# Re-timing the durations from which a two-layer transformer kernel works out each engine's order

## The reference

```python
def layer(x, c, wmod, attn, ffn):                        # twice, with different attn and ffn
    sa, ca, ga, sb, cb, gb = (silu(c) @ wmod).reshape(16, 6, 1, 128)   # per batch; ga, gb kept off 0
    x = x + ga * attn(layernorm(x) * (1 + ca) + sa)
    return x + gb * ffn(layernorm(x) * (1 + cb) + sb)

attn0(h): Q, K, V = h @ Wq + bq, ...                     # 16 heads of 8
          gate = tanh(gelu(gelu(LN(h @ dp_w1)) @ dp_w2 ...) @ g_w2)    # one number a token
          return ((softmax(causal(Q K^T * scale)) * gate) @ V) @ Wo + bo
ffn0(x):  x = x + softmax(q k^T / sqrt(128)) v @ Wo + bo               # over 128 tokens
          gates = softmax(x @ Wg + bg)                                 # 8 experts, all used
          return x + sum_e gates[e] * (relu(x @ W1[e] + b1[e]) @ W2[e] + b2[e])   # 128 -> 512 -> 128
attn1(x): q, k, v = x @ qkv_w.T;  k, v = layernorm per head
          att = q @ (k^T v / 256 * temperature + attn_bias) + x
          return gelu(att @ p1_w.T + b) @ p2_w.T + b + x
ffn1(x):  top 2 of softmax(x @ w_router); the first 1024 tokens of each expert e:
          y = gelu(x @ w1[e]) @ w2[e];  out[token] += weight * y;  return out + bias
```

## Time and profile before

| | |
|---|---|
| median of 3 runs | 1013.37 us (1011.25 to 1015.28) |
| the profiled execution | 1019.3 us, its span 1017.5 us |
| instructions | 17,056 |
| busy TensorE / VectorE / ScalarE / GpSimd | 936.2 / 608.9 / 567.8 / 347.9 us |
| granted TensorE clock, mean | 0.963 of full speed |

### The profile page before, as it was taken

How to read it: one execution, slowest core, us unless ns; L and a number is a source line. 1 busy time by engine, 2 the same in 40 slices (tenths; PEclk the granted TensorE clock), 3 DMA queues, 4 the chain that set the end, 5 groups by cost and what they waited for, 6 DMA issues and landing times.

```text
span 1017.5 us, 17056 instructions
## 1 busy us (share of the span) xinstructions
PE 936.2 (92%) x6324; PEld 628.5 (62%) x6324; DVE 608.9 (60%) x1747; ACT 567.8 (56%) x965; POOL 347.9 (34%) x436
## 2 busy tenths in 40 slices
PE   4599889888988999999999999999999998988997
PEld 3355555545656787656666566666666666877983
DVE  8988778577475675355554535554455764747334
ACT  4477876775774565445465455545555565453430
POOL 4446540330000000233424443243533323457671
PEclk9599999989997999999999999999999998998999
DMA  5865342643593000101101111111101213112316
GB/s 136 205 156 133 101 122 66 157 123 141 123 226 125 23 22 3 43 21 52 53 22 63 42 40 44 47 37 42 62 21 53 73 47 97 44 50 72 107 46 227
DMA packets 86398, 83.10 MB, mean 82 GB/s; under 512 B 9202, under 2 KB 72680, under 8 KB 86316
## 3 DMA queue, kind: packets, MB, share of 16 engines
q1 hardware_dynamic: 81092, 73.32, 26.1%
q0 software_dynamic: 4320, 8.27, 2.5%
q10 hardware_dynamic: 904, 0.42, 0.1%
HBM read 50.53 MB, written 31.72 MB: 81 GB/s over the span
## 4 chain that ended last, share of the span: by engine, by line
PE 56%; DVE 13%; issue 10%; ACT 9%; SPq 5%; POOL 5%; DMA 2%; another core or an unknown queue 0%; POOLq 0%; DVEq 0%; ACTq 0%
PE psum L1454 13%; PE psum L1487 12%; PE psum L1477 4%; PE psum L1309 4%; PE psum L1247 3%; PE psum L1263 2%; PE psum L1290 2%; POOL routed L2691 2%; SPq L1091 2%; ACT ew L2323 1%; PE psum L1217 1%; PE psum L1239 1%; POOL hT L2633 1%; DVE maxes L1844 1%; PE psum L1368 1%
## 5 line engine op out<-in xcount | busy, mean ns | idle before, releaser
L2432 ACT ACTIVATE big<-psum,cols 128x512 f32<-128x512 f32 x256 | 173.8, 689 | 162.7 <-PE psum L1454 152.1
L1454 PE MATMUL psum<-parts,q_stack 128*128 128x512 f32 x640 | 260.2, 488 | 4.2 <-issue 2.3
L1487 PE MATMUL psum<-big,ew 128*128 128x512 f32 x512 | 249.5, 595 | 0.0
L2633 POOL TENSOR_TENSOR hT<-hT,gb_tok 128x512 f32<-128x512 f32 x56 | 73.6, 1315 | 289.5 <-DVE gb_tok L1965 289.1
L1454 PEld LDWEIGHTS psum<-parts,q_stack 128*128 128x128 f32 x640 | 113.4, 194 | 61.7 <-issue 50.1
L1844 DVE TENSOR_REDUCE maxes<-psum 128x4 f32<-128x1024 f32 (+1 forms) x96 | 114.8, 1218 | 27.6 <-PE psum L1263 27.3
L1487 PEld LDWEIGHTS psum<-big,ew 128*128 128x128 f32 x512 | 96.1, 190 | 53.2 <-issue 39.9
L1454 PE MATMUL psum<-parts,k_stack 128*128 128x512 f32 x320 | 127.5, 398 | 0.0
L1965 DVE SCALAR_TENSOR_TENSOR gb_tok<-psum,cols,gb_tok 128x512 f32<-128x512 f32 x64 | 47.9, 749 | 92.4 <-PE psum L1487 84.7
L2714 POOL DMA_INDIRECT answers<-hT,to x64 | 62.5, 976 | 54.7 <-DVE hT L2163 38.0
L2691 POOL DMA_INDIRECT routed<-big,slot_i x64 | 63.2, 988 | 41.8 <-DVE slot_i L2143 22.2
(11 more groups left out here) (401 smaller groups left out, 1656.2 us busy)
## 6 DMA issues: line engine op xcount, KB each, us to landing
gb_tok<-gate_rows SPq DMA_DIRECT2D x32, 512.0 KB
q_stack<-q_pieces SPq DMA_DIRECT2D x32, 192.0 KB, 3.5
k_stack<-k_pieces SPq DMA_DIRECT2D x32, 192.0 KB, 4.5
routed<-empty_row SPq DMA_DIRECT2D x4, 1040.0 KB, 13.4
big<-routed SPq DMA_DIRECT2D x16, 260.0 KB
answers<-gb_tok SPq DMA_DIRECT2D x4, 1024.0 KB, 11.1
q_pieces<-gb_tok SPq DMA_DIRECT2D x16, 192.0 KB, 2.1
k_pieces<-gb_tok SPq DMA_DIRECT2D x15, 192.0 KB, 2.1
```

The source lines that it names most:

```text
L1454: last = eng.matmul(bank(i), w1_part(wp, e)[:, fs], parts[2 * xk + xp][:, :], start=n == 0, stop=n == 2)
L1487: eng.matmul(bank(i), ew2[:, e, f, :], hid[:, r, f, :], start=f == 0, stop=f == FC - 1).then_inc(sem("down", "pe"))
L2432: eng.activation(hid[:, held("hid", "up", n, e, f), f, :], bank(held("bank", "up", n, e, f)), ACT.Relu, bias=col("L0_ffn_b1", e * FC + f)) ...
L2633: eng.tensor_tensor(hT[:, ns], xpT[:, ns] if e == 0 else hT[:, ns], gate_wide[:, e // GHELD % 2, e % GHELD, :], ALU.add).then_inc(sem("acc ...
```

## The change

Only the `work=` durations of `order_steps()` are changed, and with them the order. Instructions, ranks, urgencies, needs and pools stay. Typical lines, and those that matter below (one line of each kind):

```diff
-        p.step("gv_g", n, work="act:2", urgent=4 if n else 8, after=[("gv_a", n)], tmp=tile)
+        p.step("gv_g", n, work="act:3.2", urgent=4 if n else 8, after=[("gv_a", n)], tmp=tile)
...
-        p.step("gv_h", n, work="act:.35", urgent=4 if n else 8, after=[("gv_d", n)], tmp=tile)
+        p.step("gv_h", n, work="act:2.9", urgent=4 if n else 8, after=[("gv_d", n)], tmp=tile)
...
-        p.step("gv_t", n, work="act:1.6", urgent=4 if n else 8, after=[("gv_r", n)])
+        p.step("gv_t", n, work="act:.35", urgent=4 if n else 8, after=[("gv_r", n)])
...
-            p.step("sg_m", l, n, work="pe:.9 act:.5", after=[("sg_r", l, n)], opens=[(0, bank)], rank=MOE - 100,
+            p.step("sg_m", l, n, work="pe:.45 act:.6", after=[("sg_r", l, n)], opens=[(0, bank)], rank=MOE - 100,
...
-                p.step("up", n, e, f, work="pe:.75 act:.6", after=[("sx", n), ("sw", 0, e), last_pv]
+                p.step("up", n, e, f, work="pe:.765 act:.72", after=[("sx", n), ("sw", 0, e), last_pv]
...
-            one("la_1", b, "pe:.43 act:.7", [("la_a", b)], rank + b, chain, kh, [ka], src=ka)
+            one("la_1", b, f"pe:.42 act:{1.75 if b % BPC == 0 else .5}", [("la_a", b)], rank + b, chain, kh, [ka], src=ka)
...
-        p.step("rt_e", g, work="act:.25", after=[("rt_s", g)], rank=rank, chain=chain)
+        p.step("rt_e", g, work="act:1.55", after=[("rt_s", g)], rank=rank, chain=chain)
...
-        p.step("rt_w", g, work="dve:1.3", after=[("rt_c", g)], rank=rank, chain=chain, urgent=1, closes=[(0, slots)], slots=slots)
+        p.step("rt_w", g, work="dve:1.75", after=[("rt_c", g)], rank=rank, chain=chain, urgent=1, closes=[(0, slots)], slots=slots)
...
-        p.step("fetch", u, work="sp:.5 dma:2.5", after=[("rt_d", b) for b in range(here)] + ([("ans", u - RINGS)] if u >= RINGS else []))
+        p.step("fetch", u, work="sp:.5 dma:3.5", after=[("rt_d", b) for b in range(here)] + ([("ans", u - RINGS)] if u >= RINGS else []))
...
-        p.step("ans", u, work="dve:1.3", after=[("down2", u, CT - 1), *[("rt_b", b) for b in range(RINGS * CHUNK // S)]]
+        p.step("ans", u, work="dve:1.75", after=[("down2", u, CT - 1), *[("rt_b", b) for b in range(RINGS * CHUNK // S)]]
```

More of the change, by code:

```diff
@@ L402, in order_steps @@
         bank = p.buffer("bank")
-        p.step("val", b, work="pe:1.2 dve:.55" if b < 4 else "pe:.75 dve:.48", urgent=6 if b < 4 else 0, after=[("ln_t", 0, 0, b), ("center",)] + ([(("proj", 0, 1), "pe")] if b < BPC else []),
+        p.step("val", b, work="pe:1.2 dve:.55" if b < 4 else "pe:.83 dve:.53", urgent=6 if b < 4 else 0, after=[("ln_t", 0, 0, b), ("center",)] + ([(("proj", 0, 1), "pe")] if b < BPC else []),
                rank=60 * (b - 3) + 4,
@@ L582, in order_steps @@
         split = p.buffer("parts")
-        p.step("sx", n, work="act:.53 dve:.62", after=[("mx_a", b) for b in range(BPC * n, BPC * n + BPC)]
+        p.step("sx", n, work="act:.6 dve:.69", after=[("mx_a", b) for b in range(BPC * n, BPC * n + BPC)]
                + ([(("up", n - 1, NE - 3, FC - 1), "pe")] if n else []),
@@ L599, in order_steps @@
                        opens=[(0, bank)] if f == 0 else [], closes=[(0, hid)] if f == FC - 1 else [], bank=bank, hid=hid)
-            p.step("mix", n, e, work="dve:.7", after=[("down", n, e, FC - 1), ("mg_r", n, e // GHELD)],
+            p.step("mix", n, e, work="dve:.78", after=[("down", n, e, FC - 1), ("mg_r", n, e // GHELD)],
                    closes=[(0, bank)], bank=bank)
-            p.step("acc", n, e, work="pool:1.25", after=[("mix", n, e)] + ([("acc", n, e - 1)] if e else []))
+            p.step("acc", n, e, work="pool:1.4", after=[("mix", n, e)] + ([("acc", n, e - 1)] if e else []))
         add_mixed(n, MOE - 300, (20 + n, -1, 0))
@@ L605, in order_steps @@
     for e in range(NE):
-        p.step("sw", 1, e, work="act:.53 dve:.62", after=[("w1",), (("up", NCH - 1, e, FC - 1), "pe")])
+        p.step("sw", 1, e, work="act:.6 dve:.69", after=[("w1",), (("up", NCH - 1, e, FC - 1), "pe")])
     for h in range(4):
@@ L632, in linear_attention @@
             chain, (kq, kk, ks, kb, ka, kh, ko) = (20 + n, b, 2), tiles[b]
-            p.step("la_m", b, work="dve:.65", after=[("la_r", n)], rank=rank + b, chain=chain, closes=[(0, ks)], src=kk)
+            p.step("la_m", b, work="dve:.93", after=[("la_r", n)], rank=rank + b, chain=chain, closes=[(0, ks)], src=kk)
             if b < B - LAST:
@@ L678, in order_steps @@
             bank = p.buffer("bank")
-            p.step("up2", u, f, work="pe:.77 act:.52", after=[("ft", u), ("sw", 1, e)] + ([(("up2", u, f - 1), "pe")] if f else []), rank=at + f,
+            p.step("up2", u, f, work=f"pe:.77 act:{1.9 if u < 2 and f == 0 else .64}", after=[("ft", u), ("sw", 1, e)] + ([(("up2", u, f - 1), "pe")] if f else []), rank=at + f,
                    opens=[(0, bank)] + ([(0, hid)] if f == 0 else []),
@@ L693, in order_steps @@
         tile = p.buffer("tmp")
-        p.step("bias", b, work="dve:.75", urgent=-20, after=[("sg_m", 1, k) for k in range(B // 4)] + [("ln_z", 1, 1, b)], chain=(92, b, 0),
+        p.step("bias", b, work="dve:1.1", urgent=-20, after=[("sg_m", 1, k) for k in range(B // 4)] + [("ln_z", 1, 1, b)], chain=(92, b, 0),
                opens=[(0, tile)], closes=[(0, tile)], tmp=tile)
```

72 lines of the change are left out of this document (36 added, 36 removed).

## The result

Over 20 runs each the changed kernel has a median of 1014.95 us (1010.27 to 1018.87) and the kernel before 1011.67 (1005.61 to 1015.28). The ratio is 1.0035, 95% interval 1.0019 to 1.0050: 3.5 us slower (1.9 to 5.1), inside half a per cent. I had forecast 1007.4, 6 us faster.

The account below looks back on a forecast made before the run. TensorE, busy 92% of the span, was taken as the bound, so an order can save only idle time. Terms 8.5 - 7 - 7 + 2.5 - 3 = -6.0 on 1013.4 gave 1007.4 us; range 999 to 1023, 8 in 10.

Parts of the forecast that it names:

- Hand-over, +8.5: From rt_c 6 to ft 0: less TensorE work covers the chain, idle 11.8 us against 3.28, so 8.5 us slower.
- Mixture, -7: Mixture stage: more cover for layer 1's chain removes most waits; of 10.3 us idle 2.5 to 3 stay, 7 us faster.
- The cover of 2.42 us: Mixture, ahead of la_2: TensorE work beside ScalarE's GELU and table load grows from 1.13 to 2.42 us; waits should vanish.
- Expert stage, -7: Behind ft 0: old stalls costing 11.1 us go, 4.1 come back at the late expert units; 7 us faster.
- the three old stalls: Expert stage, behind ft 0: stalls of 6.3 us, 11.1 with their clock, claimed to go with the new order.
- the exposed splits: Expert stage, ahead of up2 8 0: splits of ft 8 and 9 on ScalarE and VectorE uncovered for about 1 us.
- Transition, +2.5: Between attention and mixture: TensorE stops behind blk, then for mix 0 0; 2.1 us plus .4 for later gates.
- Attention, -3: Attention, 50 to 283 us: two gains of 4.8 and 4.6 against losses of 5.4 and 1, so 3 us faster.
- the 4.8 us for `mrow` 13: Attention: mrow 13 behind one weight load instead of four; its 3.20 us stall goes, 4.8 us faster with its clock.
- the waits for `exp` on ScalarE: Attention: stalls for ScalarE sum to 9.1 us; counting the table loads should remove half, 4.6 us faster.
- chunk 4's stack: Attention, from proj 4 1 to max 8 0: stack late, a new stall of 3.8 us, 5.4 with its clock.
- My rival of that sign: Slower: the hand-over isn't paid back, expert stage gives 0, sum +1; with worse attention stalls +8, 1021 us; chance .22.

Follow-up runs that it names:

- rtc6_early: Changed kernel with durations of chunk 6's linear attention and routing times 0.7 in the play: 1008.1 us beside 1010.4 for before, ratio .9985.
- la1_only: Kernel before with only la_1's duration changed, its table load counted (1.75 and .5 for .7): 1012.6 us beside 1017.7, ratio .9957.
- bias_behind: Changed kernel with bias 8 to 15 set behind ft 9, moving only VectorE's order: 1009.7 us beside 1007.6 for before, ratio 1.0012.
- before_again: Kernel before, unchanged, run again for a second profile: 1016.1 us, beside a median of 1017.9 for before in that batch.
- after_again: Changed kernel, unchanged, run again for a second profile: 1024.0 us.
- sp_true: Changed kernel with SP's issue of the eight fills at 3.8 us for .8 in the play: 1010.9 us beside 1017.7 for before, ratio .9948.
- attn_full: Kernel before with the change's durations for the attention's nine steps and ln_t: 1009.2 us beside 1010.4, ratio .9995.

## Why the prediction was wrong

- *Hand-over, +8.5*: right in mechanism and size. `rt_c` 5 to `ft` 0 is 9.4 us longer, with 12.1 idle for 3.3; no `mix` was late. Put back (rtc6_early), 7 of it return.
- *Mixture, -7*: right. Idle 3.2 us where 10.3 were; between `rt_c` 1 and 5, half of the stage's chunks, 5.3 us. What is left is nearly all a wait of `la_a` (L1568) for VectorE, which I had not named. la1_only shows that nearly all of the gain hangs on `la_1`'s duration with its table load, more than I gave it. The cover of 2.42 us was enough, and no wait of L1582 is left, as the row's 1.28 us load has it. The Trainium skill ("ScalarE: Activation LUTs", section "What ACT_TABLE_LOAD costs") gives 2.66 us for a switch with its drain. The trace does not agree: by my estimate from that figure .7 us of wait would be left in each chunk.
- *Expert stage, -7*: the step that failed. I took the three old stalls as gone (they are) and priced the new order's cost at 2.5 us and 1.6 for the clock. The new stalls are 7.9 us in one execution of the change, 12 and 13 in the other two, and the stage is as long as before (140.1, 143.1 and 149.5 us; before 140.5 and 144.2): the term is 0 or a little over. I had put the exposed splits at "about 1 us", from their own durations, and not looked at what is queued ahead of them on VectorE: four `bias` steps, 5 us. With them behind `ft` 9 (bias_behind) the wait for the splits is .5 us. The fetch was mis-sized as well, 20.7 us from `rt_c` 7 where I had 18. `rt_d` 14 waits 2.60 us for its slots where it waited 6.70, as forecast.
- *Transition, +2.5*: the mechanism was right, TensorE ahead of `mx_k` 5 waits for `mx_v` 4 behind `blk` (4.5 to 7.1 us), then for `mix` 0 0 (.6 to 1.8, not 4). No run isolates the sum, so the term stays open: all that stands ahead of `rt_c` 1 took 526.1 us in before_again and 527.1 in after_again. With its idle time gone (sp_true) the same stage is worth 11 us, more than any other.
- *Attention, -3*: attn_full gives -.5 with 2 us either way, its other expert stage included. Of its parts, the 4.8 us for `mrow` 13 were in good part an accident of one execution (3.20 us of wait there, .57 in before_again, 2.07 in la1_only, whose order is that of before up to the mixture); the waits for `exp` on ScalarE fell by 8.7 us, not by half of 9.1, but VectorE's maxima took 9 to 11.5 back, a wait that I didn't forecast; chunk 4's stack wasn't late, chunk 7's by 0 to 1.9 us.
- The sum by what was measured is -.5 for the attention, -5.3 and +9.4 for the two middle stretches and 0 for the expert stage, some 3.5 us slower with the transition left open. My rival of that sign named the right place, an expert stage that gives nothing, and would have given +1 by itself. That the attention's sum comes within 2.5 us of the forecast is luck: none of its large parts came as priced. The second error is the base: I read the terms from one profiled execution that no timed run came near.
- Two numbers of the text are off by themselves. By the cases as they stand the chances come to .38 faster, .42 same and .20 slower, not .40, .38 and .22; and behind the last `down2` 6.2 us of TensorE are idle, not 9. Neither moves the forecast.

## What to carry to other kernels

A planner's table made more truthful is no change for the better by itself: each wait moved where the order moved it, and one kind of step with durations .05 and .09 us longer was worth 13 us. What helped was finding, for each long wait, the chain that it waits for and the one duration in the play that is furthest from the trace there (most of SP's fills at .8 for 3.1 to 4.3 us, a table load left out), and setting that. When a term rests on "exposed for the length of the instruction", read what is queued ahead of that instruction on its own engine; and before summing against a profile, see that its own time lies among the timed ones.

## What the runs showed that I had not expected

The kernel's time differs from batch to batch of runs by 1% (before: 1007.6, 1010.4, 1011.7, 1017.7 and 1017.9 us in five). It isn't the chip alone: the batches of 1007.6 and 1017.7 carry the same chip's number. The expert stage with its indirect DMAs varies most (140.1 to 149.5 us for the same order, in three executions). Why, and whether the change loses more in the slow batches (ratio 1.0069 for 1.0035, the intervals overlap), stays open: in the longest one the waits beyond the splits end on ScalarE, in the next in part at "issue", and no run takes them apart.
